# The second sequence's projection moved between the first's feed-forward units, with filler matmuls for TensorE

## Chip, cores and metric

The kernel runs on one core of one Trainium2 chip. The metric is the device time of one execution in microseconds (us).

## The reference

Sixteen sequences of 512 tokens with 256 features go through two layers. Each part normalises its input and adds its result to the stream `x`:

```python
x = x + attention0(layernorm(x))          # 16 heads of 16, no bias; softmax over 512 keys in blocks of 256
x = x + ffn0(layernorm(x))                # h = xn @ W.T (+ low-rank term); relu(h)**2 @ Wp.T; 1024 hidden, ternary weights
x = x + attention1(layernorm(x))          # 16 heads, with biases
x = x + tree_ffn(layernorm(x))            # 8 trees of 255 nodes: silu(logits) on the path that the signs choose
```

`layernorm` subtracts the mean and divides by the root of variance plus 1e-5, over the 256 features. Everything is float32.

## The kernel before

Float32 products are made from pairs of float16 parts, high and low: a product takes three matmuls (`PRODUCTS`). The sequences go in eight pairs `b`. A pair has eight phases, two sequences each: 0 and 1 are the first attention of sequence 0 and 1, 2 and 3 the first feed-forward, 4 and 5 the second attention, 6 and 7 the trees. `PHASES` counts them; `x[0]` and `x[1]` hold the two streams. A phase `ph` works on sequence `ph % 2`. One layer norm precedes each phase: `stats_after` (bn_stats, L710), `moments` (seven small DVE instructions), `rstd_of` on GpSimd (POOL, L357), `normalise` (L734), `transposed` on TensorE (PE, L1008) and the read-out of the transposes as high and low parts, `hT_high` on ScalarE (ACT, L486) and `hT_low` on DVE (L739). `NORM` and `DONE` give the order of these norms and of the residual updates within a pair; all semaphore targets are computed from them.

Each engine has its instruction list written out by hand in one order, and engines meet on counting semaphores. So what stands behind a waiting instruction on the same engine waits too.

The attention of one phase is 16 steps `s`, one head each. In a step PE makes four tiles of maxima (`maxima`, L1040; for the head seven steps ahead, `LEAD`), which DVE reduces (L753 in layer 0, L756 in layer 1) from two alternating banks, `bank[0]` and `bank[1]`; four tiles of scores (`scores`, L1051), which ACT exponentiates (L524); and the product with the values of an earlier head (`weighted`, L1065). Between them stand the q, k and v units of the next phase (`qk_unit` L1020, `v_unit` L1001), row transposes of the maxima (`maxima_rows`, L1046), and in the odd phases `natural` (transposes of the attention's output, L1072; DVE then divides, L762 and L764), `attn_T` (L1077), its read-out `attn_high`/`attn_low` (L516, L770), `projected` (L1001) and `attn_residual` (L777) of the phase before. `qk_read` on ACT writes two copies of a q or k unit, `qk_low` on POOL its low part, and SP copies the parts into `qst` and `kst` (L284), six copies for each unit. The first 7 heads of a phase get their maxima ahead of it, as 14 pairs of tiles (`lead_tiles`).

The feed-forward has 16 units for a pair, `c` = 0 to 7 for sequence 0 and 8 to 15 for sequence 1. Unit `c` runs through `hidden` (six matmuls, L995) into bank 2 or 3, `relu` (ACT, L571), `square` (POOL, L382), `square_high` (ACT, L575), `square_low` (DVE, L800, for c < 8, and POOL, L386, for c >= 8), and `project` (eight matmuls, L1233), which adds into banks 4 and 5. After the eighth, `ffn_scale` (DVE, L789) and `ffn_residual` (POOL, L391) end the sequence's phase.

The order before, on PE: hidden(0) to (7) and project(0) to (7) interleaved, with the four `natural` of phase 1 among them; then `attn_T`, `projected`, the norm of phase 4, the q and k units 0 and 1 of phase 4, the norm of phase 3, v units and q and k units 2 and 3; hidden(8) to (10); and then hidden(11) to (15) and project(8) to (15) with 14 pairs of lead tiles between them, before `attention_even(b, 4)`. So sequence 0's norm for phase 4 comes ahead of sequence 1's for phase 3. A pair ends with 16 trees, interleaved with phase 0's preparation for the next pair; its last tiles are `lead_tiles` 12 and 13, and then the next pair's `attention_even(b, 0)` begins. The pieces of the opening of an even attention (`attention_even` on PE):

```python
pair_of_tiles(b, ph, n, ahead, s, 0)          # tiles 0, 1
if s >= G:
    weighted(n, ai, s // G - 1, s % G, (0,) if split else (0, 1))
pair_of_tiles(b, ph, n, ahead, s, 1)          # tiles 2, 3
```

Of the kernel before, what the change touches and what calls it, by code (L numbers as in the profile page):

```python
# [12 lines left out]
B, S, D = 16, 512, 256  # L13
T = S // P
# [5 lines left out]
NG = H // G  # L20
# [3 lines left out]
M0 = F0 // P  # L24
# [31 lines left out]
def build(nc, t, out):  # L56
    ctx = ExitStack()
    with ctx:
# [176 lines left out]

        NORM = {0: 0, 1: 1, 2: 2, 4: 3, 3: 4, 5: 5, 6: 6, 7: 7}
        DONE = {0: 0, 2: 1, 1: 2, 3: 3, 4: 4, 5: 5, 6: 6, 7: 7}
# [4 lines left out]
        N_BANK = {0: (7, 7, 7, 7), 1: (7, 0, 1, 7), 4: (7, 7, 7, 7), 5: (7, 6, 7, 6)}  # L242
# [106 lines left out]
        def _(pool):  # L349
# [78 lines left out]
            for b in range(PAIRS):  # L428
# [3 lines left out]
                for c in range(M0):  # L432
                    square(b, c)
                ffn_residual(b, 0)
                rstd_of(b, 4)
                rstd_of(b, 3)
                n2 = b * NATT + 2
                for c in range(4):
                    qk_low(n2, c)
                square(b, 8)  # L440
                square(b, 9)
                square_low(b, 8)
                for c in range(10, 15):
                    square(b, c)
                    square_low(b, c - 1)
                split_maxima(n2, 1, 0)
                square(b, 15)
                square_low(b, 14)
# [23 lines left out]
        def _(act):  # L472
# [113 lines left out]
            for b in range(PAIRS):  # L586
# [10 lines left out]
                for c in range(3, M0):  # L597
                    relu(b, c)
                    square_high(b, c - 1)
                square_high(b, M0 - 1)  # L600
                attn_high(n1, 1, 0)
                attn_high(n1, 1, 1)
                n2 = b * NATT + 2
                hT_high(b, 4, 0)
                hT_high(b, 4, 1)
                qk_read(n2, 4, 0)
                qk_read(n2, 4, 1)
                hT_high(b, 3, 0)
                hT_high(b, 3, 1)
                qk_read(n2, 4, 2)  # L610
                qk_read(n2, 4, 3)
# [3 lines left out]
                for c in range(10, UNITS):  # L615
                    relu(b, c)
                    square_high(b, c - 1)
                square_high(b, 15)
# [41 lines left out]
        def _(dve):  # L660
# [196 lines left out]
            for b in range(PAIRS):  # L857
# [6 lines left out]
                for tt in range(3):  # L864
                    natural(n1, 1, tt)
                square_low(b, 2)
                natural(n1, 1, 3)
                for c in range(3, M0):
                    square_low(b, c)
                ffn_scale(b, 0)  # L870
                attn_low(n1, 1, 0)
                attn_low(n1, 1, 1)
                stats_after(b, 2, 0)
                stats_after(b, 2, 1)
                moments(b, 4)
                attn_residual(b, 1, 0)
                attn_residual(b, 1, 1)
                normalise(b, 4)
                stats_after(b, 1, 0)
                stats_after(b, 1, 1)  # L880
                hT_low(b, 4, 0)
                hT_low(b, 4, 1)
                moments(b, 3)
                normalise(b, 3)
# [630 lines left out]
```

## Time and profile before

| | |
|---|---|
| median of 3 runs | 3384.36 us (3380.99 to 3385.28) |
| the profiled execution | 3380.93 us, its span 3379.0 us |
| mean granted clock of TensorE | 0.944 of full speed (2.4 GHz) |
| busy: PE, DVE, ACT, POOL | 3022.3, 2222.8, 1917.0, 909.1 us |

The profile is of one execution. PE is TensorE's matmuls, PEld its weight loads, SPq the queue of DMA issues. A line such as L1233 is a line of the kernel before. A granted clock of 1.00 is 2.4 GHz and 0.50 is 1.2 GHz. Matmuls overlap in the pipeline, so a row's duration has a tail of some 0.1 to 0.4 us that lies under the next row.

### The profile page before, as it was taken

The page shows a single profiled execution, that of the slowest core. Times are in us where ns is not written, and L with a number is a line of the kernel's source. Part 1 is how long each engine was busy: PE and PEld are TensorE (multiplying, and loading weights), DVE is VectorE, ACT ScalarE, POOL GpSimd, SP SyncE. Part 2 cuts the span into 40 slices and gives each one's busy share as a digit, 9 for nine tenths or more (in the row PEclk, how much of TensorE's full clock was granted, in tenths as well). Part 3 has the DMA queues.
Part 4 walks back from the last instruction along what each step waited for, and adds up shares of the span by engine and source line. Part 5 has one row for each costly group of instructions (what it writes and reads, how often), then busy time and mean ns, then how long its engine had stood idle before and what let it go on. Part 6 is the DMA issues. An engine that isn't in the chain of part 4 may idle for free.

```text
span 3379.0 us, 50607 instructions
## 1 busy us (share of the span) xinstructions
PE 3022.3 (89%) x20068; PEld 1375.3 (41%) x20068; DVE 2222.8 (66%) x4099; ACT 1917.0 (57%) x2559; POOL 909.1 (27%) x1206
## 2 busy tenths in 40 slices
PE   0488899989999899989999899998899989999899
PEld 0124255342643336333363435524254342633336
DVE  0785866758566676767667586675856667576764
ACT  0274654737547474565746566474754738456574
POOL 0013223142321414214241232314133141421413
PEclk9589899999989899998999989999899989999899
DMA  3000000000100001000010000100001000100000
GB/s 118 21 22 20 21 26 33 22 20 22 38 30 12 25 16 51 27 2 30 24 38 28 19 22 21 38 22 20 21 29 39 12 20 22 46 25 9 30 18 20
DMA packets 92700, 91.03 MB, mean 27 GB/s; under 512 B 15757, under 2 KB 89877, under 8 KB 92453
## 3 DMA queue, kind: packets, MB, share of 16 engines
q1 hardware_dynamic: 92465, 87.79, 7.6%
q8 instruction: 160, 2.62, 0.3%
q14 instruction: 75, 0.61, 0.1%
HBM read 17.48 MB, written 8.39 MB: 8 GB/s over the span
## 4 chain that ended last, share of the span: by engine, by line
PE 64%; DVE 24%; ACT 5%; SPq 3%; issue 2%; POOL 1%; DMA 1%; DVEq 0%
PE ps L995 13%; PE ps L1040 11%; PE ps L1065 10%; PE ps L1262 8%; DVE nmax L753 8%; DVE nmax L756 7%; PE ps L1020 6%; PE ps L1001 4%; PE ps L1233 3%; PE ps L1051 3%; ACT probs L524 3%; SPq L263 2%; PE ps L1008 2%; SPq L284 1%; PE ps L1253 1%
## 5 line engine op out<-in xcount | busy, mean ns | idle before, releaser
L524 ACT ACTIVATE probs<-ps 128x1024 f32<-128x1024 f32 x1024 | 1041.9, 1024 | 378.7 <-PE ps L1051 375.5
L1040 PE MATMUL ps<-kst,qst 48*128 48x512 f16 x2048 | 749.1, 409 | 145.4 <-DVE nmax L756 64.7
L753 DVE TENSOR_REDUCE nmax<-ps 128x2 f32<-128x512 f32 x1024 | 650.4, 684 | 210.9 <-PE ps L1040 204.3
L756 DVE TENSOR_REDUCE nmax<-ps 128x1 f32<-128x512 f32 x1024 | 650.3, 683 | 181.2 <-PE ps L1040 178.3
L1051 PE MATMUL ps<-qst,kst 54*128 54x512 f16 x2048 | 726.4, 406 | 5.0 <-ACT probs L524 5.0
L1065 PE MATMUL ps<-probs,vn 128*32 128x512 f32 (+1 forms) x5184 | 572.8, 515 | 6.6 <-ACT oT L512 6.6
L1040 PEld LDWEIGHTS ps<-kst,qst 48*128 48x128 f16 x2048 | 166.2, 94 | 785.0 <-DVE nmax L753 325.9
L420 POOL TENSOR_TENSOR probs<-probs 127x512 f16<-127x512 f32 (+1 forms) x256 | 292.2, 1162 | 519.7 <-ACT probs L655 519.7
L655 ACT ACTIVATE probs<-probs 127x512 f16<-127x512 f32 (+1 forms) x256 | 161.3, 630 | 350.5 <-DVE probs L949 346.8
L1262 PE MATMUL ps<-wout,probs 127*128 127x256 f16 (+1 forms) x3072 | 357.2, 273 | 0.0
L995 PE MATMUL ps<-hT,win 128*127 128x512 f16 (+1 forms) x1536 | 354.3, 380 | 2.6 <-ACT probs L631 2.6
L1262 PEld LDWEIGHTS ps<-wout,probs 127*128 127x128 f16 (+1 forms) x3072 | 297.5, 98 | 55.6 <-issue 10.7
L361 POOL TENSOR_TENSOR parts<-qk,parts 128x512 f16<-128x512 f32 x128 | 148.0, 1156 | 444.5 <-ACT qk L497 443.2
L949 DVE SCALAR_TENSOR_TENSOR probs<-ps,thr,probs 127x512 f32<-127x512 f32 (+1 forms) x256 | 179.7, 743 | 121.7 <-PE ps L1253 121.7
L367 POOL TENSOR_TENSOR npart<-nmax,zero 128x32 f16<-128x32 f32 x128 | 30.4, 238 | 793.0 <-DVE nmax L753 457.6
L995 PEld LDWEIGHTS ps<-hT,win 128*127 128x127 f16 (+1 forms) x1536 | 176.4, 117 | 162.7 <-issue 11.5
L631 ACT ACTIVATE probs<-ps,bin_ 128x512 f32<-128x512 f32 (+1 forms) x256 | 162.1, 681 | 95.1 <-PE ps L995 82.9
L1051 PEld LDWEIGHTS ps<-qst,kst 54*128 54x128 f16 x2048 | 159.5, 94 | 121.9 <-issue 79.2
L571 ACT ACTIVATE probs<-ps 128x512 f32<-128x512 f32 x128 | 76.3, 596 | 218.4 <-PE ps L995 218.2
L382 POOL TENSOR_TENSOR probs<-probs 128x512 f32<-128x512 f32 x128 | 132.6, 1039 | 221.3 <-ACT probs L571 221.3
L1065 PEld LDWEIGHTS ps<-probs,vn 128*32 128x32 f32 x5184 | 102.8, 108 | 208.8 <-issue 150.5
L995 PE MATMUL ps<-hT,wfc 128*128 128x512 f16 x768 | 184.7, 380 | 0.0
(115 smaller groups left out, 3195.9 us busy)
## 6 DMA issues: line engine op xcount, KB each, us to landing
qst<-parts SPq DMA_DIRECT2D x384, 64.0 KB, 2.6
kst<-parts SPq DMA_DIRECT2D x384, 64.0 KB, 2.6
x<-in_x SPq DMA_DIRECT2D x16, 512.0 KB, 3.6
probs<-x SPq DMA_DIRECT2D x16, 512.0 KB, 3.0
out<-probs SPq DMA_DIRECT2D x16, 512.0 KB, 3.1
qst<-nrow SPq DMA_DIRECT2D x256, 12.0 KB
qst<-in_winT SPq DMA_DIRECT2D x1, 2040.0 KB
oT<-in_wfcT SPq DMA_DIRECT2D x1, 1024.0 KB
```

Of the source, the lines that this page charges most:

```text
L420: nc.gpsimd.tensor_tensor(mlo[0:rows, a % 2, leaf, :], masked[0:rows, a % 2, leaf, :], mhi[0:rows, a % 2, leaf, :], ALU.subtract).then_inc ...
L524: nc.scalar.activation(probs[:, g % 2, 2 * hf:2 * hf + 2, s % G, :], ps[:, 2 + 2 * hf:4 + 2 * hf, :], ACT.Exp).then_inc(exp_rd, 1)
L631: nc.scalar.activation(actv[0:rows, a % 2, leaf, :], bank[2 + leaf][0:rows], ACT.Silu, scale=1.0 / WS, bias=bin_[0:rows, a % PAR, leaf:lea ...
L753: nc.vector.tensor_reduce(nmax[:, u, 2 * tt + half, :, slot], bank[tt % 2].rearrange("p (a s) -> p a s", s=BLK), AX.X, ALU.max, negate=Tru ...
L756: nc.vector.tensor_reduce(nmax[:, u, 2 * tt + half, 0, slot:slot + 1], bank[tt % 2], AX.X, ALU.max, negate=True).then_inc(max_rd, 1)
L949: nc.vector.scalar_tensor_tensor(masked[0:rows, a % 2, leaf, :], sel_at(a, leaf)[0:rows], thr[0:rows, leaf:leaf + 1], actv[0:rows, a % 2, ...
L995: ins = mm(out_ps, w[:, a, k, col:col + width], src[:, c, k, :], start=k + i == 0, stop=k == KD - 1 and i == 2)
L1020: ins = mm(out_ps, (wq, wk)[c % 2][l][:, a, k, c // 2 * P:c // 2 * P + P], hT[ph % 2][:, d, k, :], start=k + i == 0, stop=k == KD - 1 and ...
L1040: mm(bank[tt % 2], qst[lo:hi, ai % 2, e // 2, tt * P:(tt + 1) * P], kst[lo:hi, ai % 2, e // 2, :], start=True, stop=True).then_inc(max_ps, 1)
L1051: i = mm(bank[2 + kt], kst[lo:hi, ai % 2, s // 2, kt * P:(kt + 1) * P], qst[lo:hi, ai % 2, s // 2, :], start=True, stop=True)
L1065: i = mm(bank[6][32 * j:32 * j + 32, lo:hi], vn[:, ai % 2, kt, G * g + j, :], probs[:, g % 2, kt, j, lo:hi], start=kt == 0 and 0 in halves ...
L1262: i = mm(bank[4 + tt // 2][:, tt % 2 * D:(tt % 2 + 1) * D], part[0:rows, a % 2, leaf, tt * P:(tt + 1) * P], wout[0:rows, w, c, leaf, :], s ...
```

## The change

On all engines the lists of the first feed-forward are reordered. Sequence 1's `natural`, `attn_T`, `projected`, residual and norm (phase 3) come between units 1 and 8 of sequence 0. Then hidden(8) to (10), and after them the norm of phase 4. `NORM` and `DONE` become the plain order of the phases. Units 8 to 10 get their `square_low` on DVE, and project(8) to (10) and hidden(11), (12) come ahead of the lead tiles, of which some now stand four or six in a row. `keep_going(k, bank)` issues `k` matmuls of 512 columns on constants into a bank whose contents aren't needed; it waits for nothing, and nothing reads it. There are 27 of them in the feed-forward of a pair, 12 in the first two steps of phase 4, 4 in the first step of phase 0, and 9 at the end of a pair that has a successor.

```diff
@@ -232,14 +232,12 @@
-        NORM = {0: 0, 1: 1, 2: 2, 4: 3, 3: 4, 5: 5, 6: 6, 7: 7}
-        DONE = {0: 0, 2: 1, 1: 2, 3: 3, 4: 4, 5: 5, 6: 6, 7: 7}
+        NORM = DONE = {ph: ph for ph in range(PHASES)}
 ...
         V_BANK = {0: (6, 7), 1: (7, 7), 4: (0, 1), 5: (7, 7)}
-        N_BANK = {0: (7, 7, 7, 7), 1: (7, 0, 1, 7), 4: (7, 7, 7, 7), 5: (7, 6, 7, 6)}
+        N_BANK = {0: (7, 7, 7, 7), 1: (7, 0, 1, 6), 4: (7, 7, 7, 7), 5: (7, 6, 7, 6)}
         A_BANK = {0: (7, 0), 1: (0, 1), 4: (7, 0), 5: (7, 6)}
@@ -431,21 +429,27 @@
                     square(b, c)
+                rstd_of(b, 3)
                 ffn_residual(b, 0)
+                n2 = b * NATT + 2
                 rstd_of(b, 4)
-                rstd_of(b, 3)
-                n2 = b * NATT + 2
-                for c in range(4):
-                    qk_low(n2, c)
                 square(b, 8)
                 square(b, 9)
-                square_low(b, 8)
-                for c in range(10, 15):
+                square(b, 10)
+                qk_low(n2, 0)
+                qk_low(n2, 1)
+                square(b, 11)
+                qk_low(n2, 2)
+                pool.wait_ge(sq_lo, b * UNITS + 11)
+                square_low(b, 11)
+                qk_low(n2, 3)
+                square(b, 12)
+                square_low(b, 12)
+                for c in (13, 14):
                     square(b, c)
-                    square_low(b, c - 1)
+                    square_low(b, c)
                 split_maxima(n2, 1, 0)
                 square(b, 15)
-                square_low(b, 14)
                 square_low(b, 15)
@@ -594,28 +598,38 @@
                 out_read(n1, 1, NG - 1)
-                for c in range(3, M0):
-                    relu(b, c)
-                    square_high(b, c - 1)
-                square_high(b, M0 - 1)
+                relu(b, 3)
+                square_high(b, 2)
+                relu(b, 4)
+                square_high(b, 3)
                 attn_high(n1, 1, 0)
                 attn_high(n1, 1, 1)
+                square_high(b, 4)
+                for c in range(5, M0):
+                    relu(b, c)
+                    if c > 5:
+                        square_high(b, c - 1)
+                square_high(b, 7)
                 n2 = b * NATT + 2
-                hT_high(b, 4, 0)
-                hT_high(b, 4, 1)
-                qk_read(n2, 4, 0)
-                qk_read(n2, 4, 1)
                 hT_high(b, 3, 0)
                 hT_high(b, 3, 1)
-                qk_read(n2, 4, 2)
-                qk_read(n2, 4, 3)
                 relu(b, 8)
 ...
                 square_high(b, 8)
-                for c in range(10, UNITS):
+                relu(b, 10)
+                square_high(b, 9)
+                hT_high(b, 4, 0)
+                hT_high(b, 4, 1)
+                square_high(b, 10)
+                qk_read(n2, 4, 0)
+                qk_read(n2, 4, 1)
+                relu(b, 11)
+                qk_read(n2, 4, 2)
+                square_high(b, 11)
+                qk_read(n2, 4, 3)
+                for c in range(12, UNITS):
                     relu(b, c)
-                    square_high(b, c - 1)
-                square_high(b, 15)
+                    square_high(b, c)
                 row_read(n2, 0)
@@ -861,30 +875,35 @@
                 square_low(b, 1)
-                for tt in range(3):
+                for tt in range(T):
                     natural(n1, 1, tt)
                 square_low(b, 2)
-                natural(n1, 1, 3)
-                for c in range(3, M0):
-                    square_low(b, c)
-                ffn_scale(b, 0)
+                square_low(b, 3)
                 attn_low(n1, 1, 0)
                 attn_low(n1, 1, 1)
+                square_low(b, 4)
+                square_low(b, 5)
+                attn_residual(b, 1, 0)
+                attn_residual(b, 1, 1)
+                stats_after(b, 1, 0)
+                stats_after(b, 1, 1)
+                square_low(b, 6)
+                moments(b, 3)
+                square_low(b, 7)
+                normalise(b, 3)
+                ffn_scale(b, 0)
+                hT_low(b, 3, 0)
+                hT_low(b, 3, 1)
                 stats_after(b, 2, 0)
 ...
                 moments(b, 4)
-                attn_residual(b, 1, 0)
-                attn_residual(b, 1, 1)
                 normalise(b, 4)
-                stats_after(b, 1, 0)
-                stats_after(b, 1, 1)
                 hT_low(b, 4, 0)
                 hT_low(b, 4, 1)
-                moments(b, 3)
-                normalise(b, 3)
+                square_low(b, 8)
+                square_low(b, 9)
+                square_low(b, 10)
                 n2 = b * NATT + 2
-                hT_low(b, 3, 0)
-                hT_low(b, 3, 1)
                 values(n2, 4, 0)
@@ -1082,6 +1101,11 @@
+            def keep_going(k, free):
+                for _ in range(k):
+                    mm(free, idb[:], wfc[:, HI, 0, 0:S], start=True, stop=True)
@@ -1110,7 +1134,11 @@
                         weighted(n, ai, s // G - 1, s % G, (0,) if split else (0, 1))
+                    if s == 0 or (s == 1 and nxt == 5):
+                        keep_going(4, bank[6])
                     pair_of_tiles(b, ph, n, ahead, s, 1)
+                    if s == 0 and nxt == 5:
+                        keep_going(4, bank[6])
                     if split:
@@ -1301,46 +1329,53 @@
                 hidden(b, 3)
+                pe.wait_ge(oT_sb, n1 * NG + NG)
+                for tt in range(T):
+                    natural(n1, 1, tt)
                 project(b, 1)
-                pe.wait_ge(oT_sb, n1 * NG + NG)
-                natural(n1, 1, 0)
-                natural(n1, 1, 1)
-                natural(n1, 1, 2)
                 hidden(b, 4)
                 project(b, 2)
-                pe.wait_ge(attn_sb, n1 * T + 1)
-                natural(n1, 1, 3)
-                for c in range(5, M0):
-                    hidden(b, c)
-                    project(b, c - 2)
-                project(b, 6)
-                project(b, 7)
                 pe.wait_ge(attn_sb, n1 * T + T)
 ...
                 attn_T(n1, 1, 1)
+                hidden(b, 5)
+                project(b, 3)
                 pe.wait_ge(aT_hi, n1 * KD + KD)
 ...
                 projected(n1, 1, 1)
+                hidden(b, 6)
+                project(b, 4)
+                hidden(b, 7)
+                project(b, 5)
+                project(b, 6)
+                project(b, 7)
+                keep_going(3, bank[1])
+                transposed(b, 3, 0)
+                transposed(b, 3, 1)
+                keep_going(4, bank[1])
+                hidden(b, 8)
+                hidden(b, 9)
+                hidden(b, 10)
+                keep_going(6, bank[1])
                 transposed(b, 4, 0)
                 transposed(b, 4, 1)
+                keep_going(8, bank[4])
                 hT_read(b, 4, 0)
 ...
                 qk_unit(n2, 4, 1)
-                transposed(b, 3, 0)
-                transposed(b, 3, 1)
+                project(b, 8)
                 pe.wait_ge(qk_sb, n2 * 4 + 1)
 ...
                 v_unit(n2, 4, 1)
-                hT_read(b, 3, 0)
+                hidden(b, 11)
+                project(b, 9)
                 qk_unit(n2, 4, 2)
-                hT_read(b, 3, 1)
                 qk_unit(n2, 4, 3)
-                hidden(b, 8)
-                hidden(b, 9)
-                hidden(b, 10)
+                project(b, 10)
+                hidden(b, 12)
                 lead = [(e, tt) for e in range(LEAD) for tt in (0, 2)]
@@ -1350,20 +1385,30 @@
                 lead_tiles(n2, 2, 0)
+                project(b, 11)
                 lead_tiles(n2, 2, 1)
-                project(b, 8)
-                for c in range(11, UNITS):
-                    lead_tiles(n2, 2, 2 * (c - 11) + 2)
-                    hidden(b, c)
-                    lead_tiles(n2, 2, 2 * (c - 11) + 3)
-                    project(b, c - 2)
-                    if c == UNITS - 1:
-                        pe.wait_ge(qk_sb, n2 * 4 + 4)
-                        maxima_rows(n2, 0)
+                hidden(b, 13)
+                lead_tiles(n2, 2, 2)
+                project(b, 12)
+                lead_tiles(n2, 2, 3)
+                hidden(b, 14)
+                lead_tiles(n2, 2, 4)
+                lead_tiles(n2, 2, 5)
+                project(b, 13)
+                lead_tiles(n2, 2, 6)
+                lead_tiles(n2, 2, 7)
+                hidden(b, 15)
+                lead_tiles(n2, 2, 8)
+                lead_tiles(n2, 2, 9)
+                project(b, 14)
+                lead_tiles(n2, 2, 10)
+                pe.wait_ge(qk_sb, n2 * 4 + 4)
+                maxima_rows(n2, 0)
+                lead_tiles(n2, 2, 11)
                 lead_tiles(n2, 2, 12)
-                project(b, 14)
+                project(b, 15)
+                keep_going(6, bank[2])
                 lead_tiles(n2, 2, 13)
-                project(b, 15)
                 attention_even(b, 4)
@@ -1441,8 +1486,11 @@
                 if more:
+                    keep_going(2, bank[6])
                     lead_tiles(n4, 0, 12)
+                    keep_going(4, bank[6])
                     lead_tiles(n4, 0, 13)
+                    keep_going(3, bank[6])
                 pe.wait_ge(x_upd, (b + 1) * (2 * PHASES))
```

## Rows read from the trace of the kernel before

**Rows 1.** The page: busy time, and the granted clock in the 40 slices (tenths of full speed).

```profile
PE 3022.3 (89%) x20068; PEld 1375.3 (41%) x20068; DVE 2222.8 (66%) x4099; ACT 1917.0 (57%) x2559; POOL 909.1 (27%) x1206
...
PEclk9589899999989899998999989999899989999899
```

**Rows 2.** Windows; columns: length, busy us and count of each engine, clock, DMA.

```profile
1115.05:1121.88 6.83, 5.33 (x18) 2.44 (x17) 4.42 (x16) 2.33 (x4) 1.01 (x1) 0.50 0.01 2
...
1159.42:1176.49 17.07, 13.42 (x48) 3.92 (x46) 14.03 (x33) 9.96 (x11) 2.48 (x6) 0.50 0.01 3
1384.70:1388.12 3.42, 3.37 (x14) 1.80 (x14) 1.57 (x3) 2.49 (x4) 0.98 (x4) 0.50 0.00 0
...
1391.53:1401.77 10.24, 9.24 (x28) 2.16 (x28) 5.04 (x8) 5.47 (x7) 1.15 (x1) 0.50 0.12 42
```

**Rows 3.** Timeline of PE in the feed-forward: start, us, engine, line; wait before in brackets.

```profile
1089.32 1.05 PE L1233 MATMUL ps<-wpt,probs 128*128 128x256 f16 x8
...
1105.45 1.92 PE L1233 MATMUL ps<-wpt,probs 128*128 128x256 f16 x16 [1.19 <-DVE probs L800]
...
1109.90 2.78 PE L1001 MATMUL ps<-wo,hT 128*128 128x256 f16 x24 [1.66 <-DVE hT L770]
1114.76 1.73 PE L1008 MATMUL ps<-idf,h 128*128 128x128 f32 x8 [2.07 <-DVE h L734]
1117.99 2.72 PE L1020 MATMUL ps<-hT,wq 128*128 128x512 f16 x6 [1.50 <-DVE hT L739]
...
1122.48 1.04 PE L1008 MATMUL ps<-idf,h 128*128 128x128 f32 x8
...
1125.98 1.46 PE L1020 MATMUL ps<-hT,wq 128*128 128x512 f16 x6
...
1128.57 4.05 PE L995 MATMUL ps<-hT,wfc 128*128 128x512 f16 x18
```

**Rows 4.** Line 800 (ns: min/median/max), and two rows of DVE's timeline.

```profile
L800 DVE TENSOR_TENSOR probs<-probs x64: 679/1111/1115, 282.1 to 3119.1; 128x512 f16<-128x512 f32 x64
...
1109.68 1.39 DVE L710 BATCH_NORM_STATS2 stats<-x 128x6 f32<-128x256 f32 x4
...
1113.33 1.37 DVE L734 TENSOR_SCALAR h<-x,mean,rstd 128x256 f32<-128x256 f32 x4
```

**Rows 5.** Timeline of POOL: ffn_residual and rstd_of.

```profile
1107.74 2.49 POOL L391 TENSOR_TENSOR x<-probs,x 128x512 f32<-128x512 f32 x2 [2.90 <-DVE probs L789]
1112.04 1.02 POOL L357 TENSOR_TENSOR rstd<-vpe,mhalf 128x4 f32<-128x4 f32 x1 [1.82 <-DVE vpe L729]
```

**Rows 6.** Timeline of SP's queue: the copies of the first k unit.

```profile
1125.29 3.77 SPq L284 DMA_DIRECT2D kst<-parts  x6
```

**Rows 7.** Timeline of PE: lead tiles between the second sequence's units.

```profile
1132.55 0.60 PE L1040 MATMUL ps<-kst,qst 48*128 48x512 f16 x2
...
1134.64 1.05 PE L1233 MATMUL ps<-wpt,probs 128*128 128x256 f16 x8
...
1136.15 1.47 PE L995 MATMUL ps<-hT,wfc 128*128 128x512 f16 x6
1137.55 0.60 PE L1040 MATMUL ps<-kst,qst 48*128 48x512 f16 x2
1138.09 1.05 PE L1233 MATMUL ps<-wpt,probs 128*128 128x256 f16 x8
1139.07 0.64 PE L1040 MATMUL ps<-kst,qst 48*128 48x512 f16 x2
...
1158.69 0.37 PE L1040 MATMUL ps<-kst,qst 48*128 48x512 f16 x1 [1.63 <-DVE nmax L756]
```

**Rows 8.** DVE at the openings: its timeline, and its waits from 1157 to 1180.

```profile
1157.87 2.53 DVE L756 TENSOR_REDUCE nmax<-ps 128x1 f32<-128x512 f32 x4
...
DVE nmax L756 <- PE ps L1040: 3.6, 4, 2.0
...
1380.98 5.11 DVE L753 TENSOR_REDUCE nmax<-ps 128x2 f32<-128x512 f32 x8
```

## The prediction

> **What bounds the kernel now.** I read the page first: TensorE (PE) is busy for 89% of the span, DVE for 66%, no other engine for more than 57% [rows 1], so a gain must come out of PE's stream or of what PE waits for. Two things show. The granted clock is not level [rows 1], and the windows of one pair say where it falls to 0.50, that is 1.2 instead of 2.4 GHz [rows 2]: once in the norm between the two feed-forwards (6.83 us long, PE busy 5.33), once at the opening of the second layer's first attention (17.07, busy 13.42), twice at the opening of the next pair (3.42 and 10.24, busy 3.37 and 9.24). Each fall comes behind a thin stretch. Then the timeline of PE in the feed-forward [rows 3]: waits of 1.19 us before project(6), 1.66 before projected, 2.07 before the transposes of the norm, 1.50 before the first q unit. They are one serial path (project(7), scale, residual, statistics, rstd, normalise, transposes, read-out), and nothing but half-speed work lies beside it. All further times are of that pair, the third of eight; the slices of the page repeat from pair to pair [rows 1].
>
> **The change, step by step.**
>
> (a) The feed-forward up to project(7). In front of it now stand attn_T and projected of the second sequence: 8 transposes and 24 matmuls, 0.9 + 2.6 us (a row of 8 takes 1.04 with its tail, one of 24 2.78 [rows 3]). By order of issue project(5) ends near 1106.9 (before: about 1104.1; some 0.8 us of small waits there is filled). Then project(6) needs DVE's square_low(6), and DVE's queue holds ahead of it square_low(5) (to 1105.95; ScalarE reads square 5 only after relu(6), which waits for hidden(6)), two residual steps at 0.6 and four bn_stats at 1.3 [rows 4]: 1109.15. So PE waits 2.3 us, where it waited 1.19. The moments (0.8) and square_low(7) (0.7) make it wait 0.6 more, and project(7) ends at 1111.6; before it ended at 1107.2 (start 1105.45, two at 0.88 [rows 3]). **+4.4 us.**
>
> (b) From project(7) to the first q unit. DVE: normalise(3) until 1112.5, ffn_scale until 1113.7; POOL's second residual half ends at 1115.6 (1.24 each [rows 5]); bn_stats of that half 1116.5, moments 1117.3, rstd 1.02 on POOL [rows 5] 1118.4, normalise 1.37 [rows 4] 1119.9, transposes 1120.9. ScalarE's hT_high(4) stands behind square_high(8), relu(10) and square_high(9), and square 8 comes on POOL only after rstd: 1122.4, hT_low 1123.3. So the q unit starts at 1123.3, not 1117.99: **+5.3**. But hidden(8) to (10) (4.0 at full clock) and the transposes of the other norm (0.9) are done by then, and the half clock that cost 5.33 × 0.5 = 2.65 before is spared if the fillers hold it.
>
> (c) The 21 fillers up to here: 512 columns each, priced at a row of the same shape, 4.05 us for 18 [rows 3], so about 0.22 and 4.6 together. They lie in waits of about 0.9, 1.1, 1.5 and 2.4 us, for normalise(3), its read-out, normalise(4) and its read-out: nothing on the path. Were those waits shorter than I have them, the fillers would cost up to their 4.6 us; if a wait is longer they are free.
>
> (d) 1123.3 to the first lead tile: four q/k units 5.2, two v units 2.6, hidden(11), (12) 2.7, project(8) to (10) 2.7: 1136.5 (before 1132.55). SP's queue: the six copies of a unit take 3.77 us to issue [rows 6]; two units from 1125.5 on, and a landing, give 1135.7, so the tiles do not wait, by 0.8 us. POOL loses three square_lows to DVE, which has room: they run 0.68 alone and 1.11 beside a POOL square [rows 4], 3.3 us at most before values at 1128.5.
>
> (e) The lead. Before, 14 tile pairs were spread between ten units of PE work; a pair takes 0.54 there, project 0.98, hidden 1.40 [rows 7], and DVE (0.6 per tile) kept up. Now h13 to h15 and p11 to p15 are left for it: 14 × 0.54 + 5 × 0.98 + 3 × 1.40 + row transposes 0.33 = 17.0. Four tiles in a row take 2.09 instead of 1.07 [rows 7], since two banks wait for DVE: three times +1.0, the six tiles around the row transposes +1.7, and 0.4 for square_low(12), behind qk_low(3) on POOL: 22.1, less the last pair: project(15) ends at 1158.1 (before 1157.06). Six fillers (1.3) stand behind it beside ffn_scale (1.2), then the last pair. DVE's first tile of the next attention comes at 1160.85, where it came at 1159.1 (third of the first four in [rows 8]). **(a) to (e): +1.75 us per pair.** The serial path is filled, and the lead becomes DVE's instead.
>
> (f) Opening of the second layer's attention. DVE starts on four tiles at 1157.87 and has 3.6 us of waits for PE until 1180, in four pieces, the longest 2.0 [rows 8]; in the rest it works, half clock or not. Full speed can give back the short ones up to the q unit, 1.4. The long one holds a q unit that takes 2.72 at half clock against 1.46 [rows 3]. The 12 fillers lie beside bn_stats, moments and normalise: nothing, or, did DVE wait for the tiles behind them, 2.6. They stop after s = 1, and s = 2 and 3 stay as thin as before, so I take it that the clock still falls once, later and shorter, over part of that unit: 0.6 gained out of 1.25. **−2.0.**
>
> (g) Opening of the next pair (seven times). 9 + 4 fillers. DVE reduces eight tiles without a pause from 1380.98 on, 5.11 us [rows 8], so most lie in waits; 0.4 of 2.8 us is taken as cost (bounds 0 and 2.8). The first fall goes: its busy 3.37 [rows 2] could give 1.7, but DVE covers about half of it: 0.9 gained. The second one (busy 9.24, worth at most 4.6, but DVE paces the tiles: 2.7) follows on s = 1, where no filler stands; I take half, 1.3. **−1.8.**
>
> What would make the clock hold has no row here; its price is bounded by the same stretches: none of it gained, or all.
>
> **Sum:** 8 × (1.75 − 2.0) + 7 × (−1.8) = −14.6 us. The profiled execution took 3380.93 (span 3379.0), 3.4 under the median shown; 3380.93 − 14.6 = 3366.3, put at the median 3369.7, and given as 3369.
>
> **One rule weighed against a row.** DVE's square_low took 1.11 us, against 0.68 alone [rows 4], where it started inside a POOL square. The Trainium skill, SBUF — State Buffer, "Who interferes with whom", says that a DVE instruction with two SBUF inputs contends with a GpSimd one that reads SBUF, and that the port pair they share is an exclusive lock. By rows, the three moved to DVE cost 3.3 us; by that rule a wait behind a whole square is possible, about 1.7 each, 5.2 in all. It would end at 1128.5, just where values is due: the sum stays, its cover would be gone.
>
> **Rivals.** *The clock is lost in the new wait (slower).* Behind project(5) PE now waits 2.3 us and 0.6 us; before, the fall at 1115.05 followed waits of 1.19, 1.66 and 2.07 within ten us [rows 3]. If it falls there, project(6), (7) and the fillers run at half speed, about +1.3; the row transposes of the lead, with six tiles around, are the second such place (project(15) and six fillers, +1.3). It decides from 2.0 us on: with either one, and the two openings giving only 1.4 and 0.5, a pair is +1.6 (7 × 0.5 for the openings): 8 × (1.75 + 1.3 − 1.4) − 3.5 = +9.7, about 3394. Against it: project(4) and (5) just before are dense. *The clock holds everywhere (faster).* Then (f) gives 2.65 and (g) 3.2: 8 × (1.75 − 2.65) − 7 × 3.2 = −30, 3355. For it: fillers stand at each place where it fell. Against it: the s where none stands. *Nothing happens:* the thin s still lose the clock, the openings are DVE's, and the +1.75 eats what they give: 3380 to 3388.
>
> **How the numbers follow.** My case 0.34, the clock holds 0.22, nothing 0.17, the clock is lost 0.27. A change within 0.2% (7 us) cannot be told from none here. My case and the full one give faster, with a tenth of the slow and quiet ones moved there if the chain in (a), (b) is shorter than walked: faster 0.56, same 0.18, slower 0.26. Range: 3355 less another 1.3 us per pair for a shorter walk, 3344; upwards 3394 with a bit of the fillers uncovered, 3399. The likeliest case alone: 3358 to 3378.
>
> **What would show it.** In the changed profile: project(6) of each pair waits about 2 us for DVE's L800; the q unit of the second layer starts some 5 us later after the first project than now (1117.99 − 1089.32 = 28.7 us [rows 3]), with full clock there; the first L1051 of that attention comes 71 us after the first project (now 1158.69 − 1089.32 = 69.4 [rows 7]); half-clock stretches at s = 2 to 3, not at s = 0; the first fall of the next pair's opening gone. If the time from first project to that L1051 is shorter than now, (a) to (e) are wrong; if no 0.5 is left in a pair, (f) and (g) are too low.

## The result, and the profile after

| | before | changed |
|---|---|---|
| median | 3384.22 us | 3426.52 us |
| ratio, 95% interval | | 1.0129 (1.0111 to 1.0146) |
| profiled execution, span | 3380.93, 3379.0 | 3427.66, 3425.8 |
| mean granted clock | 0.944 | 0.957 |

The change made the kernel 42 us slower, where 15 us less was forecast, and the range (up to 3399) does not hold the time. The clock is better than before; the time is not. The page of the changed kernel (compare [rows 1]):

```profile
PE 3096.6 (90%) x20475; PEld 1413.0 (41%) x20475; DVE 2250.5 (66%) x4123; ACT 1919.5 (56%) x2559; POOL 891.8 (26%) x1182
...
PEclk9589899999999999998999999999999989999899
```

To find the place I cut each pair at eight events, read off the timelines: the first project matmul (P0), project(6) (P6), end of project(7) (P7), first q unit of phase 4 (Q), first lead tile (L), end of project(15) (P15), first scores of phase 4 (A), first v unit behind them (V); then the same two of the next pair's phase 0 (A0, V0). The two ends are taken without a row's tail, as the start of the last matmul and 0.1 us. Means over the pairs in us, in brackets the half-clock time in each stretch:

```
             P0-P6   P6-P7      P7-Q        Q-L         L-P15       P15-A      A-V          V-A0    A0-V0        V0-P0
before       16.13   1.75       10.62(2.3)  14.64(4.1)  24.33       1.81       26.30(17.1)  198.16  25.96(14.6)  82.96
walked       19.9    2.4        11.7        13.2        21.6        2.2        24.3         -       24.2         -
changed      19.55   2.75(1.6)  14.12(1.7)  13.15       23.44(7.8)  3.90(2.4)  25.74(6.8)   198.84  23.47(5.4)   83.00
```

The walked row is the prediction's own times, taken as differences (its V terms as before less what was forecast). P0 to A takes 76.90 us instead of 69.30 (forecast 71), 8 × 7.6 = 61 us; the two openings give back 0.56 and 2.49 us and V to A0 costs 0.68: 61 − 8 × 0.56 − 7 × (2.49 − 0.68) = 44, and the first pair reaches P0 2.3 us later: 46 of the 46.8 us between the spans. Against the walked times P0 to A is 5.9 us a pair too long, 47 us in all, and that lies in P7–Q (2.4), L–P15 (1.8) and P15–A (1.7). The opening A–V is another 1.4 us a pair over, 12 us in all.

The third pair of the changed kernel, timeline of PE, against [rows 3, 7]. L1261 is project, L1014 hidden, L1107 the fillers, L1027 the transposes of a norm, L1039 a q or k unit, L1070 scores:

```profile
1101.82 1.05 PE L1261 MATMUL ps<-wpt,probs 128*128 128x256 f16 x8
...
1118.26 1.05 PE L1261 MATMUL ps<-wpt,probs 128*128 128x256 f16 x8 [0.19 <-DVE probs L814]
1121.36 3.56 PE L1261 MATMUL ps<-wpt,probs 128*128 128x256 f16 x16 [2.06 <-DVE probs L814]
...
1127.51 4.04 PE L1014 MATMUL ps<-hT,wfc 128*128 128x512 f16 x18 [0.20 <-DVE hT L753]
1131.40 1.46 PE L1107 MATMUL ps<-wfc,idb 128*128 128x512 f16 x6
1134.90 1.92 PE L1027 MATMUL ps<-idf,h 128*128 128x128 f32 x8 [2.05 <-DVE h L748]
1136.62 2.78 PE L1107 MATMUL ps<-wfc,idb 128*128 128x512 f16 x8
1139.24 1.46 PE L1039 MATMUL ps<-hT,wq 128*128 128x512 f16 x6
...
1172.50 1.88 PE L1261 MATMUL ps<-wpt,probs 128*128 128x256 f16 x8
1174.16 2.35 PE L1107 MATMUL ps<-wfc,idb 128*128 128x512 f16 x6
...
1177.71 0.39 PE L1070 MATMUL ps<-qst,kst 54*128 54x512 f16 x1
```

Project(6) waits 2.06 us, as walked (2.3). Then project(6) and (7), 16 matmuls, take 3.56 us and not 1.92. The transposes of phase 4's norm still wait 2.05 us with six fillers in front of them; so that wait was not filled, it was some 3.4 us long. DVE and POOL show why:

```profile
1119.33 1.39 DVE L724 BATCH_NORM_STATS2 stats<-x 128x6 f32<-128x256 f32 x4
1120.64 0.67 DVE L814 TENSOR_TENSOR probs<-probs 128x512 f16<-128x512 f32 x1
...
1123.58 1.38 DVE L748 TENSOR_SCALAR h<-x,mean,rstd 128x256 f32<-128x256 f32 x4 [0.90 <-POOL rstd L355]
...
1131.31 3.54 DVE L748 TENSOR_SCALAR h<-x,mean,rstd 128x256 f32<-128x256 f32 x4 [1.13 <-POOL rstd L355]
1136.64 0.69 DVE L753 TENSOR_TENSOR hT<-ps,hT 128x512 f16<-128x512 f32 x1 [1.79 <-ACT hT L490]
```

```profile
1130.26 1.02 POOL L355 TENSOR_TENSOR rstd<-vpe,mhalf 128x4 f32<-128x4 f32 x1 [2.11 <-DVE vpe L743]
1131.25 2.09 POOL L380 TENSOR_TENSOR probs<-probs 128x512 f32<-128x512 f32 x2
1133.51 1.19 POOL L380 TENSOR_TENSOR probs<-probs 128x512 f32<-128x512 f32 x1 [0.18 <-ACT probs L575]
```

Normalise, four instructions of L748, took 1.38 us in phase 3 and 3.54 in phase 4. POOL's rstd ended at 1131.3, and its squares of units 8, 9 and 10 ran from 1131.25 to 1134.70, beside the second one. In the kernel before those squares came after the v units, and the same four took 1.37 [rows 4]. Windows, columns as in [rows 2]: project(6) and (7), the lead of pair 3, the opening of phase 4, and the lead of pair 4:

```profile
1121.60:1125.00 3.40, 3.40 (x18) 2.36 (x17) 2.46 (x10) 0.00 (x0) 1.39 (x1) 0.54 0.00 0
1152.30:1174.20 21.90, 18.44 (x90) 7.64 (x90) 16.93 (x27) 5.50 (x9) 11.14 (x14) 0.96 0.09 31
1189.86:1196.69 6.83, 6.58 (x24) 1.26 (x22) 3.97 (x7) 4.23 (x5) 1.06 (x1) 0.52 0.04 12
1556.00:1583.00 27.00, 24.77 (x98) 9.10 (x96) 17.36 (x27) 6.54 (x11) 12.60 (x16) 0.73 0.09 32
```

### The profile page after: what moved, and what is told of

Its sections match the earlier page's. It is cut to its first block, busy times and chain, and to the rows that moved or that the text cites. A ratio compares the mean times of both kernels' runs of the same rounds, so it can differ in the third digit from the quotient of the medians.

```text
span 3425.8 us, 51413 instructions
## 1 busy us (share of the span) xinstructions
PE 3096.6 (90%) x20475; PEld 1413.0 (41%) x20475; DVE 2250.5 (66%) x4123; ACT 1919.5 (56%) x2559; POOL 891.8 (26%) x1182
## 3 DMA queue, kind: packets, MB, share of 16 engines
q8 instruction: 163, 2.67, 0.3%
## 4 chain that ended last, share of the span: by engine, by line
PE 61%; DVE 25%; ACT 5%; SPq 4%; issue 2%; POOL 2%; DMA 1%; DVEq 0%
PE ps L1014 12%; PE ps L1059 10%; PE ps L1084 10%; DVE nmax L770 9%; PE ps L1290 8%; DVE nmax L767 7%; PE ps L1039 5%; PE ps L1020 4%; PE ps L1261 3%; ACT probs L528 3%; PE ps L1070 3%; SPq L261 2%; PE ps L1107 2%; DVE h L748 2%; SPq L282 1%
## 5 line engine op out<-in xcount | busy, mean ns | idle before, releaser
L1059 PE MATMUL ps<-kst,qst 48*128 48x512 f16 x2048 | 735.0, 401 | 135.0 <-DVE nmax L770 56.8
L1070 PE MATMUL ps<-qst,kst 54*128 54x512 f16 x2048 | 698.4, 392 | 5.0 <-ACT probs L528 5.0
L1014 PE MATMUL ps<-hT,win 128*127 128x512 f16 (+1 forms) x1536 | 354.3, 380 | 2.7 <-ACT probs L645 2.7
L1014 PEld LDWEIGHTS ps<-hT,win 128*127 128x127 f16 (+1 forms) x1536 | 176.5, 117 | 162.7 <-issue 11.5
L1070 PEld LDWEIGHTS ps<-qst,kst 54*128 54x128 f16 x2048 | 157.9, 93 | 121.9 <-issue 79.2
L1014 PE MATMUL ps<-hT,wfc 128*128 128x512 f16 x768 | 189.6, 387 | 1.6 <-DVE hT L753 1.6
```

The costliest lines, as they stand in the source:

```text
L1014: ins = mm(out_ps, w[:, a, k, col:col + width], src[:, c, k, :], start=k + i == 0, stop=k == KD - 1 and i == 2)
L1059: mm(bank[tt % 2], qst[lo:hi, ai % 2, e // 2, tt * P:(tt + 1) * P], kst[lo:hi, ai % 2, e // 2, :], start=True, stop=True).then_inc(max_ps, 1)
L1070: i = mm(bank[2 + kt], kst[lo:hi, ai % 2, s // 2, kt * P:(kt + 1) * P], qst[lo:hi, ai % 2, s // 2, :], start=True, stop=True)
```

## The experiments

Each is told by its difference to the kernel named. All times are medians; the kernel before ran at 3381.1 to 3382.5 beside them. Measured, with the ratio to the kernel before and its 95% interval:

| run | us | ratio | P0–Q | L–P15 | P15–A | P0–V |
|---|---|---|---|---|---|---|
| changed kernel | 3426.52 | 1.0129 (1.0111 to 1.0146) | 36.42 | 23.44 | 3.90 | 102.64 |
| e1_no_fillers | 3415.75 | 1.0100 (1.0085 to 1.0115) | 35.25 | 22.69 | 1.81 | 100.59 |
| e8_opening_fillers_only | 3397.12 | 1.0050 (1.0035 to 1.0065) | 35.07 | 22.84 | 1.82 | 98.56 |
| e3_square_after_norm | 3422.58 | 1.0121 (1.0098 to 1.0143) | 35.39 | 23.48 | 4.07 | 101.64 |
| e13_act_order_only | 3419.92 | 1.0113 (1.0098 to 1.0128) | 36.26 | 22.79 | 4.05 | 101.19 |
| e5_norm_alone | 3388.28 | 1.0017 (1.0008 to 1.0027) | 33.46 | 21.53 | 3.80 | 97.53 |
| e4_low6_first | 3424.17 | 1.0125 (1.0109 to 1.0140) | 36.27 | 23.14 | 4.16 | 101.44 |
| e7_lead_spread | 3393.73 | 1.0039 (1.0025 to 1.0053) | 36.13 | 22.07 | 2.67 | 98.03 |
| e9_alone_and_spread | 3364.44 | 0.9954 (0.9939 to 0.9969) | 33.35 | 21.49 | 2.67 | 94.49 |
| e10_no_last_six | 3361.17 | 0.9939 (0.9924 to 0.9954) | 33.41 | 21.68 | 1.89 | 94.83 |
| kernel before | 3384.22 | 1 | 28.51 | 24.33 | 1.81 | 95.59 |
| e2_before_next_pair | 3368.00 | 0.9958 (0.9943 to 0.9973) | 28.25 | 24.54 | 1.81 | 95.51 |
| e6_before_both_openings | 3361.01 | 0.9943 (0.9926 to 0.9959) | 28.44 | 24.53 | 1.81 | 94.91 |
| e11b_thin_steps_filled | 3359.77 | 0.9939 (0.9922 to 0.9955) | 28.26 | 24.34 | 1.81 | 94.82 |
| e12_before_norm_filled | 3350.50 | 0.9905 (0.9891 to 0.9920) | 28.21 | 24.34 | 1.81 | 93.30 |
| e14_best | 3338.73 | 0.9875 (0.9858 to 0.9891) | 28.20 | 24.33 | 1.81 | 93.14 |

**Fillers or order.** e1 takes all fillers out, e8 only the 27 of the feed-forward.

```diff
-                keep_going(8, bank[4])
...
-                keep_going(6, bank[2])
```

(and the three others of the feed-forward; in e1 `keep_going` issues none.)

> The changed kernel with every filler matmul taken out, all reordering kept; the result is the reference's. Theory A (the reordered chain costs, the fillers lie mostly in waits and pay at the next pair's opening): about 2.1 us per pair come back in the feed-forward (8 of 21 and the last 6 are not covered in full), but the opening of the next pair loses its 2.5 us and the clock falls where it fell before: 3415 to 3440, within 0.4% of the changed kernel's 3426.5. Theory B (the fillers are the cost, 52 x 0.22 = 11 us per pair less what waits hide): below 3395. With A, the q unit of the second layer still starts 35 us or more after the first project (37.4 in the changed kernel, 28.7 before).

> The changed kernel without the 27 fillers of the feed-forward, with the 25 of the two openings. If the feed-forward's fillers are what costs and the openings' are what gains: e1_no_fillers' 3415.8 less 7 x 1.5 to 2.5 us: 3398 to 3406. If the feed-forward's fillers hold the clock where it would fall: 3420 or more.

Theory A held in both. The order alone costs 33 us over the kernel before (e1). The openings' fillers then gain 18.6 (e8 to e1), and the feed-forward's fillers cost 29 (changed to e8): of 3.7 us a pair, 1.35 lie in P0–Q and 2.1 in P15–A, where the last six stand before tiles that DVE waits for.

**The normalise beside the squares.** e3 holds POOL, e13 changes ScalarE's order alone, e5 does both.

```diff
+                pool.wait_ge(ln_h, (b * PHASES + NORM[4]) * T + T)      # e3, e5
                 square(b, 8)
...
                 relu(b, 9)
-                square_high(b, 8)
                 relu(b, 10)
-                square_high(b, 9)
                 hT_high(b, 4, 0)
                 hT_high(b, 4, 1)
+                square_high(b, 8)                                        # e5, e13
+                square_high(b, 9)
                 square_high(b, 10)
```

> The changed kernel, with GpSimd's squares 8 to 10 held until DVE's four normalise instructions of phase 4 are done. Theory A (those four took 3.54 us in the changed kernel and 1.37 before because the squares run beside them): they take 1.4 again and the transposes behind them come 2.2 us earlier, 8 x 2.2 = 17 us: 3405 to 3413. Rival (the long normalise hides behind the other waits, or the squares, later now, hold hT_high on ScalarE by as much): 3422 to 3428.

> As e3_square_after_norm, and on ScalarE hT_high(4) stands ahead of square_high(8) and (9), so the later squares no longer hold it. Theory (the shared-port stretch of normalise(4), 3.54 against 1.38 us, is on the path, and in e3 it was only handed on to ScalarE's queue): from project(7) to the q unit 11.5 to 12 us, where the changed kernel took 14.1 and e3 13.3, 2 us per pair, 3398 to 3410. Rival (eight fillers and the rest of the path fill the same time): 3418 to 3424.

> The changed kernel with only ScalarE's order changed: hT_high(4) ahead of square_high(8) and (9), the squares still beside normalise(4). Theory (the stretched normalise is the cost, and ScalarE's queue only inherits it once the squares are held): hT_high waits for the transposes anyway, project(7) to the q unit stays at 13.5 us or more, and the time at 3420 to 3428. Rival (ScalarE's order alone was the cost): 3388 to 3400, with the q unit 11.5 to 12 us behind project(7).

e3's own gain is small: its rival held. e13 came at the edge of its theory (3419.9 for 3420 to 3428), far from its rival. Timelines of DVE and of ScalarE in e3 (L580 square_high, L576 relu, L491 hT_high):

```profile
1129.45 1.38 DVE L749 TENSOR_SCALAR h<-x,mean,rstd 128x256 f32<-128x256 f32 x4 [1.13 <-POOL rstd L355]
1134.14 1.29 DVE L754 TENSOR_TENSOR hT<-ps,hT 128x512 f16<-128x512 f32 x2 [3.30 <-ACT hT L491]
```

```profile
1131.99 0.63 ACT L580 ACTIVATE probs<-probs 128x512 f16<-128x512 f32 x1 [2.94 <-POOL probs L380]
1132.52 0.58 ACT L576 ACTIVATE probs<-ps 128x512 f32<-128x512 f32 x1
1133.00 0.62 ACT L580 ACTIVATE probs<-probs 128x512 f16<-128x512 f32 x1
1133.52 1.07 ACT L491 ACTIVATE hT<-ps 128x512 f16<-128x512 f32 x2
```

Normalise takes 1.38 again, but hT_high(4) starts only at 1133.52, so DVE waits 3.30 us for it behind the normalise, where e13 below shows 1.38: square_high(8), relu(10) and square_high(9) stand ahead of it and now wait for the squares. In e13 the stretch is still there and the read-out follows the transposes at once:

```profile
1126.81 3.54 DVE L748 TENSOR_SCALAR h<-x,mean,rstd 128x256 f32<-128x256 f32 x4 [1.13 <-POOL rstd L355]
1131.73 1.29 DVE L753 TENSOR_TENSOR hT<-ps,hT 128x512 f16<-128x512 f32 x2 [1.38 <-ACT hT L490]
```

With both, e5, the q unit starts 11.33 us behind project(7) on the mean, 2.8 less than in the changed kernel (DVE's normalise, then PE):

```profile
1118.69 1.38 DVE L749 TENSOR_SCALAR h<-x,mean,rstd 128x256 f32<-128x256 f32 x4 [1.13 <-POOL rstd L355]
...
1120.12 1.09 PE L1028 MATMUL ps<-idf,h 128*128 128x128 f32 x8
1121.06 1.89 PE L1108 MATMUL ps<-wfc,idb 128*128 128x512 f16 x8
1122.88 1.46 PE L1040 MATMUL ps<-hT,wq 128*128 128x512 f16 x6
```

So either edit alone is handed to the other, and both together gave 38 us, more than the 16 to 28 expected. 8 × 2.8 = 22 of them lie in P7–Q. The rest is mostly in L–P15 (23.44 to 21.53), whose instructions were not touched: the lead then began at another moment, and the clock fell in it for 1.2 us a pair instead of 7.8. That this follows from the moment is argued, not shown.

**The long wait before project(6).**

```diff
                 attn_residual(b, 1, 1)
+                square_low(b, 6)
                 stats_after(b, 1, 0)
                 stats_after(b, 1, 1)
-                square_low(b, 6)
```

> The changed kernel, with DVE's square_low(6) ahead of the four bn_stats of phase 3, so project(6) waits 0.7 us and not 2.06. Theory A (the long wait costs itself and the fall of the clock behind it, which makes project(6), (7) and fillers run at 1.2 GHz): 1.3 us plus 1 to 1.5 us per pair, 3405 to 3416, and no 0.50 between project(5) and the transposes of phase 3. Rival (the chain through normalise(3) and project(7) ends no earlier, since the statistics are only moved behind): 3420 to 3428 with the same start of the q unit.

The rival held. The clock no longer falls there (0.1 us of half clock in P6–P7, and 1.6 in the changed kernel), yet the waits only moved, to 1.12 and 1.77 us, and P0 to P7 is 22.4 as before; DVE is the chain there in both orders:

```profile
1121.74 1.05 PE L1261 MATMUL ps<-wpt,probs 128*128 128x256 f16 x8 [1.12 <-DVE probs L814]
1124.55 1.05 PE L1261 MATMUL ps<-wpt,probs 128*128 128x256 f16 x8 [1.77 <-DVE probs L814]
...
1126.83 1.09 PE L1027 MATMUL ps<-idf,h 128*128 128x128 f32 x8 [0.59 <-DVE h L748]
```

**The lead.** e7 puts hidden(12) and project(10) back among the tiles, with no more than two pairs in a row; e9 is e7 with e5's edits, e10 is e9 without the last six fillers.

```diff
                 lead_tiles(n2, 2, 0)
+                project(b, 10)
                 lead_tiles(n2, 2, 1)
+                hidden(b, 12)
                 lead_tiles(n2, 2, 2)
...
                 project(b, 15)
-                keep_going(6, bank[2])          # e10
                 lead_tiles(n2, 2, 13)
```

> The changed kernel with hidden(12) and project(10) put back among the lead tiles, and at most two tile pairs in a row. Theory (four and six tiles in a row make PE wait for DVE and let the clock fall): from the first lead tile to project(15) starts 2.2 us earlier and ends 1.5 to 2 us earlier, and the clock falls there in none of the pairs, which gives another 2 us on average: 3394 to 3412. Rival (the tiles now wait for the copies of the k unit, so nothing is won): 3420 to 3428, with waits for DMA of kst or qst of over 1 us per pair.

> The changed kernel with both edits that helped alone: e5_norm_alone (normalise(4) without the squares beside it, hT_high(4) first) took 38 us off, e7_lead_spread 33. Theory (two separate places on one path, so they add up but for what the clock gives twice): 3355 to 3368, below the kernel before; the time from the first project to the first v unit of the second layer's opening near 94.5 us (95.6 before, 102.6 in the changed kernel). Rival (with the q unit 2.5 us earlier the spread lead tiles wait for the copies of the k unit, or both edits gave the same half-clock time): 3375 to 3390.

> e9 without the six fillers between project(15) and the last pair of lead tiles. Theory (they stand in front of tiles that DVE needs, so about 0.9 of their 1.3 us is on the path): project(15) to first scores 1.8 us instead of 2.7, 7 us less than e9 in all. Rival (without them the clock falls at the opening, as in the kernel before): within 2 us of e9 or above it.

e7 and e9 came as the theory said, but for one thing in e7: the clock still fell in the lead in three pairs of eight, for 3.4 us each. In the changed kernel four pairs of eight lose the clock in the lead for 14 us, and these take 25.0 to 25.2 us from L to P15, the other four 21.7; this is pair 4, with hidden(15) and project(14), (15) at half speed:

```profile
1563.30 1.47 PE L1014 MATMUL ps<-hT,wfc 128*128 128x512 f16 x6
...
1570.08 2.74 PE L1014 MATMUL ps<-hT,wfc 128*128 128x512 f16 x6
...
1575.28 1.89 PE L1261 MATMUL ps<-wpt,probs 128*128 128x256 f16 x8
...
1581.12 1.89 PE L1261 MATMUL ps<-wpt,probs 128*128 128x256 f16 x8
1582.80 2.77 PE L1107 MATMUL ps<-wfc,idb 128*128 128x512 f16 x6
```

e9 has no half clock from P0 to A at all. e10 gained 3.3 us of the 7 expected: P15–A fell by 0.8, and the clock fell for longer behind it (8.4 us in A–V, and 3.8 in e9). Even so mended, the new order takes 69.1 us from P0 to A, where the kernel before takes 69.3: of the waits that it was to fill, next to nothing came back as time.

**Fillers on the order of before.** e2 has the 9 + 4 of the next pair's opening, e6 also the 12 of phase 4, e11b 13 more in the thin steps, e12 has e6's and 14 in the norm of phase 4, and e14 is e12 with e11b's five of phase 0:

```diff
                 projected(n1, 1, 1)
+                keep_going(8, bank[2])          # e12, e14
                 transposed(b, 4, 0)
                 transposed(b, 4, 1)
+                keep_going(6, bank[2])          # e12, e14
...
                         hT_read(b, nxt, 0)
+                        keep_going(5, bank[7])  # e11b, e14: step 1 of phase 0
                         maxima_rows(n, 1)
```

> The kernel before, with only the 9 fillers at a pair's end and the 4 in the first step of phase 0. Theory A: this part alone gains what the two traces show there, 2.5 us in each of seven openings, 17 us: 3367, with the first half-clock stretch of that opening gone and the second one cut from 10.2 us to about 3.4. Rival (the stretch shortened by the place where the changed kernel happens to stand when the clock falls, not by the fillers): 3380 to 3390.

> The kernel before with the fillers of both openings: those of e2_before_next_pair and the 12 in the first two steps of phase 4. Theory (in the second layer's opening DVE is the bound and two later steps stay thin, so the clock falls once all the same): the opening from first scores to first v unit goes from 26.3 to 25 us at best, 3358 to 3368 in all. Rival (the fillers there cost as much as they give, as the changed kernel's 25.7 with a later start says): 3368 to 3374.

> The kernel before with the fillers of both openings (e6) and 13 more in the thin steps behind them: 5 in step 1 of phase 0, 4 each in steps 2 and 3 of phase 4. Theory (the clock falls because those steps hold little but tiles): no 0.50 left in either opening, which gives 1.0 to 1.5 us each, less what of the fillers is uncovered: 3345 to 3358. Rival (DVE paces those steps and the fillers delay its tiles): 3361 to 3372.

> The kernel before with the fillers of both openings (e6) and 14 in the norm of phase 4: 8 in the wait of 2.07 us before its transposes, 6 in the wait of 1.50 before the first q unit. Theory (the clock falls there in the kernel before and costs about half of a busy 5.3 us): the time from first project to first lead tile goes from 43.1 to 41 us and the half-clock 6 us there vanish: 3340 to 3352. Rival (14 fillers of 0.22 outlast the waits, or the clock falls elsewhere): 3356 to 3366.

> e12_before_norm_filled (the order of before, fillers in both openings and in the norm of phase 4) with the five fillers of e11b in step 1 of phase 0. Theory (they take away the last fall of the clock in the next pair's opening, 23.4 to 21.8 us in e11b): 7 x 1.2 = 8 us off, 3338 to 3345. Rival (the clock then falls at another place of the pair): 3346 to 3354.

Each fell as its theory said but e11b, which held in half: A0–V0 fell from 22.91 to 21.84 with no half clock left, while A–V rose from 25.50 to 26.08. The rise lies in three pairs, which took 27.0 to 28.2 us with 6.8 to 10.2 of half clock; the other five took 25.2 to 25.4. So what cost was the clock, and why it fell for longer in those three is open. e14 takes the good half. Its norm in the third pair (L1088 fillers, L1008 transposes, L1020 the q unit), against [rows 3], and windows over the feed-forward and the next opening:

```profile
1100.24 2.78 PE L1001 MATMUL ps<-wo,hT 128*128 128x256 f16 x24 [1.66 <-DVE hT L770]
1102.86 1.89 PE L1088 MATMUL ps<-wfc,idb 128*128 128x512 f16 x8
1105.09 1.09 PE L1008 MATMUL ps<-idf,h 128*128 128x128 f32 x8 [0.34 <-DVE h L734]
1106.02 1.46 PE L1088 MATMUL ps<-wfc,idb 128*128 128x512 f16 x6
1107.85 1.46 PE L1020 MATMUL ps<-hT,wq 128*128 128x512 f16 x6 [0.37 <-DVE hT L739]
```

```profile
1086.00:1130.00 44.00, 39.00 (x238) 22.20 (x238) 26.17 (x59) 17.00 (x31) 20.79 (x19) 1.00 0.11 37
1379.00:1402.00 23.00, 20.92 (x165) 7.01 (x164) 18.22 (x30) 18.99 (x24) 4.07 (x10) 1.00 0.11 37
```

The transposes take 1.09 and the q unit 1.46 us where they took 1.73 and 2.72. e14 beats both kernels: 3338.73 us, ratio 0.9875. It takes 67.6 us from P0 to A, less than any kernel with the new order.

## Why the prediction was wrong

Two steps failed: the normalise of (b), and the half clock from project(6) to the first scores, which my case had at nothing.

(a) Right: project(6) waits 2.06 (2.3 given), P0 to the end of project(7) is 22.3, as walked. It hits 22.3 with some luck: P0–P6 is 0.35 shorter than walked, and the rival's fall of the clock makes up for it. That fall came in four pairs of eight (P6–P7 3.2 to 3.3 us, 2.2 in those without), a mean of 0.5 us, though the wait before it was the same in all eight. What is serial there is DVE, and in e4 the other order of its work won nothing.

(b) Wrong, the first step that failed: "normalise 1.37 [rows 4] 1119.9". The row was taken from a moment when POOL stood idle; the change starts POOL's squares 8 to 10 in that very stretch, and in every pair the four DVE instructions took 3.54. I had weighed that contention for square_low alone and not for normalise, though the kernel before held it:

```profile
L734 DVE TENSOR_SCALAR h<-x,mean,rstd x256: 399/406/1247, 133.3 to 3313.8; 128x256 f32<-128x256 f32 x128
```

There the norms of phases 0 and 1 took 2.62 and 3.05 us for the same four instructions in every pair but the first, beside POOL's L420. In the three pairs of the changed kernel with no half clock from P0 to Q, P7–Q is 13.7 us: 2.0 over the 11.7 walked. In e5, with the normalise at 1.38, it is 11.3. The half clock, in which eight fillers stand behind the late transposes (c), adds the rest to 14.1; over P6–Q it costs 0.9 us on the mean. "Nothing on the path" for the 21 fillers was off by 1.35 us (changed to e8).

(d) Right: 13.15 us (13.2).

(e) The second step that failed: the sum has no half clock. Without it L–P15 takes 21.0 (pair 6 of e5, the same order of tiles and no half clock there; 21.6 walked) and P15–A 2.67 (e9, with the six fillers; 2.2 walked). The changed kernel took 23.44 and 3.90, so the half clock costs about 2.4 and 1.2 us a pair there. That it falls in the lead stood in the rival, at 1.3 us; in half of the pairs it costs 3.5 in L–P15. The tiles in a row are not the whole of it: spread tiles (e7) took most of that half clock away, and so did e5, which left the tiles as they were. What exactly makes the clock fall stays open. Of the 3.90, 2.1 come with the last six fillers (e8).

(f) Half right: DVE's short waits up to the q unit went, and A to the q unit fell from 15.1 to 13.9 us, 1.2 of the 1.4 expected. But the q unit still ran at half clock in the third pair, now with the `weighted` behind it, and DVE's long wait stayed:

```profile
1191.53 2.72 PE L1039 MATMUL ps<-hT,wq 128*128 128x512 f16 x6
...
1194.82 1.29 DVE L770 TENSOR_REDUCE nmax<-ps 128x1 f32<-128x512 f32 x2 [2.24 <-PE ps L1059]
```

The q unit to V took 11.8 us, and 11.2 before, so the 0.6 gained there became 0.7 lost, and A–V took 25.74 us where 24.3 was walked. On the order of before, the same 12 fillers gave 0.9 (e2 to e6).

(g) Right in sign and size, 2.49 less 0.68 at the pair's end against 1.8, in part by luck: the gain was put at 2.2 and the cost at 0.4. On the order of before the same fillers gave 2.57 (e2), but e1, with none, also has 24.89 in A0–V0 and not 25.96, with 12.7 us of half clock for 14.6.

One sum of the chances is off: 0.56 for faster is 0.34 and 0.22 without the tenth of the others that the text moves there, which makes 0.60.

So the slower rival named both places of the clock, sized the first about right (1.1 us in P6–P7 where it fell, up to 1.9 by Q, for 1.3) and the second at a third; the stretched normalise was in none of the cases. The rule that I weighed was the right one on the wrong instruction: the three `square_low` moved to DVE took 0.68 us each. The Trainium skill, SBUF — State Buffer, "Who interferes with whom", lists `tensor_scalar` among those whose fast modes take the port pair that DVE shares with GpSimd. By that rule the four normalise instructions can each wait behind a square. The trace agrees for three of the four: these took 1.12 to 1.13 us, and the one that began between two squares 0.40, which makes 3.54 against 1.38 us.

## What to carry to other kernels

A duration is a row at one moment: when a step moves, ask what the neighbour engine does in the stretch where it lands, and read the group's maximum, not only its median. Fillers pay where they are placed in a wait (e14, 1.25%; the openings' on the new order 18.6 us) and cost where they stand before work that is due (the feed-forward's on the new order, 29 us). A better mean clock is not a better time: 0.957 and 3426.5 us here, 0.944 and 3384.2 before. And an edit that frees one engine is handed to the next queue: e3 and e13 gave 4 and 7 us, both together 38.

## What was not expected of the hardware

The time of untouched stretches depends on when they begin: L–P15 of one kernel took 21.7 or 25.2 us in different pairs, by how long the granted clock was down in it. e4, which changes one step of the feed-forward, has 24.72 us in A–V and 24.90 in A0–V0, where the changed kernel has 25.74 and 23.47; so a single stretch, or a single pair, can mislead, and means over the pairs are compared here. And of the contention DVE bore nearly all: its four instructions went from 1.38 to 3.54 us, while POOL's three squares beside them took 1.04, 1.09 and 1.19 us, and 1.04 where it is alone.
